# Thresholds and evaluations of its own for the second attention step of a four-layer graph network

## The reference

```python
S = adj + I;  Rf = S / rowsum(S);  Rb = S / colsum(S)[:, None]
Xf = Xb = Xa = X
for s in range(2):                       # the two attention steps
    logits = (Xa @ W1) @ W2 @ (Xa @ W3).T              # 3327 x 3327
    # row by row: keep the largest logits until their softmax mass reaches 0.9,
    # the softmax of these alone is A
    A = softmax(where(keep_top_mass(logits, 0.9), logits, -inf))
    Xf, Xb, Xa = Rf @ Xf, Rb @ Xb, A @ Xa
    Z += Xf @ U1[s] + Xb @ U2[s] + Xa @ U3[s]
out = layernorm(X + Z) * gamma + beta
```

## Time and profile before

| | us |
|---|---|
| median of three runs | 3657.98 |
| the profiled execution | 3658.36 |
| its span, first to last instruction | 3656.6 |
| busy: TensorE / VectorE / ScalarE / GpSimd | 3177.0 / 2622.1 / 1892.0 / 927.5 |

### The profile page before, as it was taken

The page is one execution under the profiler, slowest core; times in us unless marked ns, Lnnn a source line. Parts: engine busy times, 40 slices in busy tenths (PEclk is TensorE's granted clock), DMA queues, the critical chain, the costliest instruction groups (busy, mean ns, idle before and its releaser), DMA issues. The chain is left out here.

```text
span 3656.6 us, 40405 instructions
## 1 busy us (share of the span) xinstructions
PE 3177.0 (87%) x13264; PEld 2292.1 (63%) x13264; DVE 2622.1 (72%) x3768; ACT 1892.0 (52%) x2355; POOL 927.5 (25%) x2293
## 2 busy tenths in 40 slices
PE   4999899987999999989875887668799899996799
PEld 3788688875677676767642444334455555554588
DVE  6963400005989989998839999999999999999100
ACT  2211311117788787878744564546466566563100
POOL 1212411111122121221202233224233333234211
PEclk9999999988999999999987998889899999998899
DMA  6644444432122121222221111111122221222255
GB/s 246 216 156 135 129 152 156 156 116 65 52 66 61 55 67 56 60 57 60 63 71 40 55 48 45 49 35 54 46 80 57 76 80 58 76 76 79 73 191 178
DMA packets 142415, 328.48 MB, mean 90 GB/s; under 512 B 15456, under 2 KB 95392, under 8 KB 130976
## 3 DMA queue, kind: packets, MB, share of 16 engines
q1 hardware_dynamic: 142240, 326.31, 28.1%
HBM read 287.59 MB, written 38.67 MB: 89 GB/s over the span
## 5 line engine op out<-in xcount | busy, mean ns | idle before, releaser
L1345 DVE SCALAR_TENSOR_TENSOR U<-E,trial 128x3327 f32<-128x3327 f32 x208 | 777.7, 3739 | 0.2 <-issue 0.2
L878 PE MATMUL bank<-Hc,PT 128*128 128x256 f32 x2704 | 635.8, 387 | 53.8 <-ACT PT L1060 53.8
L878 PEld LDWEIGHTS bank<-Hc,PT 128*128 128x128 f32 x2704 | 520.5, 194 | 176.7 <-ACT PT L1060 77.5
L918 PE MATMUL bank<-big,adj 128*128 128x512 f32 x1352 | 612.3, 604 | 0.0
L1020 ACT ACTIVATE junk<-E,neg_c 128x3327 uint8<-128x3327 f32 x156 | 479.1, 3071 | 5.1
L1020 ACT ACTIVATE junk<-E,neg_3c 128x3327 uint8<-128x3327 f32 x156 | 478.3, 3066 | 0.0
L891 PE MATMUL tr<-ident,E 128*128 128x128 f32 x1352 | 203.7, 294 | 309.4 <-DVE E L1394 309.4
L918 PEld LDWEIGHTS bank<-big,adj 128*128 128x128 f32 x1352 | 254.7, 194 | 330.0 <-issue 327.4
L1060 ACT ACTIVATE PT<-tr 128x1024 f32<-128x1024 f32 x208 | 177.7, 854 | 472.2 <-PE tr L891 471.5
L891 PEld LDWEIGHTS tr<-ident,E 128*128 128x128 f32 x1352 | 174.8, 152 | 340.1 <-DVE E L1394 322.2
L918 PE MATMUL bank<-Hc,adj 128*128 128x256 f32 x1352 | 319.5, 388 | 1.2 <-ACT bias L1041 1.2
(11 more groups left out here) (232 smaller groups left out, 4424.1 us busy)
## 6 DMA issues: line engine op xcount, KB each, us to landing
adj<-adjT SPq DMA_DIRECT2D x131, 448.0 KB, 3.4
E<-adjT SPq DMA_DIRECT2D x32, 1664.0 KB, 6.9
adj<-adjT SPq DMA_DIRECT2D x104, 384.0 KB, 3.3
adj<-adjT SPq DMA_DIRECT2D x20, 1664.0 KB, 7.0
adj<-adjT SPq DMA_DIRECT2D x14, 1216.0 KB, 5.7
E<-adjT SPq DMA_DIRECT2D x13, 1216.0 KB, 5.7
xt<-xin SPq DMA_DIRECT2D x52, 128.0 KB, 5.5
x_d<-xn SPq DMA_DIRECT2D x52, 128.0 KB, 1.7
```

What stands on the lines that cost most here:

```text
L878: last = mm(axp[:, 0:D], PT[k % 2][:, h, i * P:(i + 1) * P], Hc[:, j], start=(k == 0 and h == 0 and i == 0), stop=(k == SLOTS - 1 and h == ...
L918: last = mm(agg[:, 0:w], adj[:, j], rhs[:, j], start=(j == 0), stop=False)
L1345: V_.scalar_tensor_tensor(out=U[:, 0:N], in0=e, scalar=point, in1=e, op0=ALU.is_ge, op1=ALU.mult, accum_out=found))
```

## The change

Step 2 gets fixed thresholds of its own, four in place of the shared three; it evaluates four times in place of five, and it aims at 4 elements short of the target in place of 3. Step 1 keeps its thresholds, evaluations and aim. The small tables of `bracket` exist once for each step.

```diff
-EVALS = (3, 5)
+EVALS = (3, 4)
-AIM = 3.0
+AIM = (3.0, 4.0)
-FIXED = (0.008, 0.03, 0.1)
-NF = len(FIXED)
+FIXED = ((0.008, 0.03, 0.1), (0.0029, 0.0064, 0.0142, 0.0315))
+NFS = tuple(len(f) for f in FIXED)
+SPLIT = ((0, 1, 3, 5, 6), (0, 2, 4, 7, 8))
...
+            summed = lambda t: 2 * (NFS[0] * min(t, NT) + NFS[1] * max(t - NT, 0))
...
                         def fixed(t, lo, hi):
-                            sums = [(func, c, acc_) for c in range(NF) for func, acc_ in ((ACT.Relu, over), (ACT.Sign, sign))]
+                            step = t // NT
+                            sums = [(func, c, acc_) for c in range(NFS[step])
+                                    for func, acc_ in ((ACT.Relu, over), (ACT.Sign, sign))]
...
-                                    fixed(F, 0, 1)
+                                    fixed(F, *SPLIT[F // NT][0:2])
...
-                                        fixed(F, 1, 3)
+                                        fixed(F, *SPLIT[F // NT][1:3])
...
-                                        fixed(F, 3, 5)
+                                        fixed(F, *SPLIT[F // NT][2:4])
...
-                                        fixed(F, 5, 2 * NF)
+                                        fixed(F, *SPLIT[F // NT][3:5])
...
-                            pool.wait_ge(fixed_done, 2 * NF * (t + 1))
+                            pool.wait_ge(fixed_done, summed(t + 1))
...
-                                then(V_.tensor_scalar(sc[:, 0:1], point, AIM, tgt, ALU.mult, ALU.subtract),
+                                then(V_.tensor_scalar(sc[:, 0:1], point, AIM[step], tgt, ALU.mult, ALU.subtract),
```

More of the change, by code:

```diff
@@ L660, in build @@
             rz = ab("rz", [P, 4])
[L661 to L671, removed]
+            over = ab("over", [P, 2, max(NFS)])
+            sign = ab("sign", [P, 2, max(NFS)])
+            neg_c = [ab(f"neg_c{r}", [P, n]) for r, n in enumerate(NFS)]
+            neg_3c = [ab(f"neg_3c{r}", [P, n]) for r, n in enumerate(NFS)]
+            half_c = [ab(f"half_c{r}", [P, n]) for r, n in enumerate(NFS)]
+            half_nc = [ab(f"half_nc{r}", [P, n]) for r, n in enumerate(NFS)]
+            table = [ab(f"table{r}", [P, n + 2, 3]) for r, n in enumerate(NFS)]
+            ft = [ab(f"ft{r}", [P, 2, n]) for r, n in enumerate(NFS)]
+            met = [ab(f"met{r}", [P, n + 2]) for r, n in enumerate(NFS)]
+            pick = [ab(f"pick{r}", [P, n + 1]) for r, n in enumerate(NFS)]
+            both = [ab(f"both{r}", [P, 2, n + 1, 3]) for r, n in enumerate(NFS)]
             share = ab("share", [P, 5])
@@ L1013, in fixed @@
                         def fixed(t, lo, hi):
-                            sums = [(func, c, acc_) for c in range(NF) for func, acc_ in ((ACT.Relu, over), (ACT.Sign, sign))]
+                            step = t // NT
+                            sums = [(func, c, acc_) for c in range(NFS[step])
+                                    for func, acc_ in ((ACT.Relu, over), (ACT.Sign, sign))]
                             for m in range(lo, hi):
                                 func, c, acc_ = sums[m]
-                                if 2 * NF * t + m >= 1:
-                                    act.wait_ge(fixed_done, 2 * NF * t + m)
-                                less, scale = (neg_3c, 3.0) if func == ACT.Sign else (neg_c, 1.0)
+                                if summed(t) + m >= 1:
+                                    act.wait_ge(fixed_done, summed(t) + m)
+                                less, scale = (neg_3c[step], 3.0) if func == ACT.Sign else (neg_c[step], 1.0)
                                 go(junk[:, 0:N], E[:, t % 3, 0:N], func, bias=less[:, c:c + 1], scale=scale,
@@ L1161, in _ @@
                         tt = G_.tensor_tensor
[L1162 to L1167, removed]
+                        values = []
+                        for r in range(2):
+                            n = NFS[r]
+                            values += [(table[r][:, 0], 0.0), (table[r][:, n + 1, 0:1], 1.5), (table[r][:, n + 1, 1:3], 0.0),
+                                       (met[r][:, 0:1], 1.0), (met[r][:, n + 1:n + 2], 0.0)]
+                            for i, value in enumerate(FIXED[r]):
+                                c, _ = between_floats(value)
+                                values += [(table[r][:, i + 1, 0:1], c), (half_c[r][:, i:i + 1], c / 2),
+                                           (half_nc[r][:, i:i + 1], c * N / 2)]
                         for i, value in enumerate((P_NUC, 1 - P_NUC, -P_NUC, -1.0, 1 - 2.0 ** -24)):
@@ L1175, in bracket @@
                         def bracket(t):
-                            par = t % 2
+                            par, step = t % 2, t // NT
+                            NF = NFS[step]
                             n = [0]
@@ L1186, in bracket @@
                             lo, hi = ends2[:, par, 0], ends2[:, par, 1]
-                            mid = table[:, 1:NF + 1]
-                            pool.wait_ge(fixed_done, 2 * NF * (t + 1))
+                            mid = table[step][:, 1:NF + 1]
+                            pool.wait_ge(fixed_done, summed(t + 1))
                             if t >= 2:
                                 pool.wait_ge(probs_ready, t - 1)
-                            then(tt(ft[:, 0], sign[:, par], half_c[:], ALU.mult),
-                                 tt(ft[:, 1], over[:, par], half_nc[:], ALU.add),
+                            then(tt(ft[step][:, 0], sign[:, par, 0:NF], half_c[step][:], ALU.mult),
+                                 tt(ft[step][:, 1], over[:, par, 0:NF], half_nc[step][:], ALU.add),
@@ L1194, in bracket @@
                                  tt(tgt, Zs[:, par:par + 1], share[:, 0:1], ALU.mult),
-                                 tt(table[:, 0, 1:2], Zs[:, par:par + 1], share[:, 1:2], ALU.mult),
-                                 tt(table[:, NF + 1, 1:2], Zs[:, par:par + 1], share[:, 2:3], ALU.mult))
-                            then(tt(mid[:, :, 2], ft[:, 0], ft[:, 1], ALU.add))
+                                 tt(table[step][:, 0, 1:2], Zs[:, par:par + 1], share[:, 1:2], ALU.mult),
+                                 tt(table[step][:, NF + 1, 1:2], Zs[:, par:par + 1], share[:, 2:3], ALU.mult))
@@ L1198, in bracket @@
+                            then(tt(mid[:, :, 2], ft[step][:, 0], ft[step][:, 1], ALU.add))
                             then(tt(mid[:, :, 1], mid[:, :, 2], tgt.to_broadcast([P, NF]), ALU.subtract),
                                  tt(below, tgt, share[:, 4:5], ALU.mult),
-                                 G_.tensor_scalar(met[:, 1:NF + 1], mid[:, :, 2], tgt, None, ALU.is_ge))
+                                 G_.tensor_scalar(met[step][:, 1:NF + 1], mid[:, :, 2], tgt, None, ALU.is_ge))
                             for i in range(2, NF + 1):
-                                then(tt(met[:, i:i + 1], met[:, i:i + 1], met[:, i - 1:i], ALU.mult))
@@ L1203, in bracket @@
[L1203 to L1207, removed]
+                                then(tt(met[step][:, i:i + 1], met[step][:, i:i + 1], met[step][:, i - 1:i], ALU.mult))
+                            then(tt(pick[step][:], met[step][:, 0:NF + 1], met[step][:, 1:NF + 2], ALU.subtract))
@@ L1208, in bracket @@
+                            w = pick[step][:].unsqueeze(2).to_broadcast([P, NF + 1, 3])
+                            then(tt(both[step][:, 0], table[step][:, 0:NF + 1], w, ALU.mult),
+                                 tt(both[step][:, 1], table[step][:, 1:NF + 2], w, ALU.mult))
                             for i in range(1, NF):
-                                then(tt(both[:, :, 0], both[:, :, 0], both[:, :, i], ALU.add))
-                            then(tt(ends2[:, par], both[:, :, 0], both[:, :, NF], ALU.add))
+                                then(tt(both[step][:, :, 0], both[step][:, :, 0], both[step][:, :, i], ALU.add))
@@ L1212, in bracket @@
+                            then(tt(ends2[:, par], both[step][:, :, 0], both[step][:, :, NF], ALU.add))
                             then(tt(sp_[:, 0:1], lo[:, 1:2], hi[:, 1:2], ALU.subtract),
@@ L1294, in _ @@
                         V_.memset(ones8[:], 1.0)
[L1295 to L1298, removed]
+                        for r in range(2):
+                            for i, value in enumerate(FIXED[r]):
+                                c, three_c = between_floats(value)
+                                V_.memset(neg_c[r][:, i:i + 1], -c)
+                                V_.memset(neg_3c[r][:, i:i + 1], -three_c)
                         V_.memset(flag[:], 0.0).then_inc(search, 1)
```

## The result

The changed kernel takes **3735.6 us** (median of 4 runs, 3730.05 to 3737.45) against 3658.45 before: a ratio of **1.0208**, 95% interval 1.0195 to 1.0221. It is slower by 77 us, where 60 us faster was forecast. The profiled execution is the shortest of the four, 3730.05 us, so the sums taken from its trace come to about 72 us and not 77.

A forecast was written before the change was run, and what follows sets the result against it. VectorE was taken to bound step 2, with GpSimd's bracket close behind. −137 evaluations + 69 waits + 7 start + 3 collision = −58, −60 after rounding: 3658 − 60 = 3598 us, range 3564 to 3642.

The forecast's parts named there:

- The number of rounds: Extraction-loop rounds in step 2, taken as unchanged at 51; forecast case 45 to 58, about −94 us at 45, −20 at 57.
- Rival 1: Four evaluations leave rows needing more extraction rounds in step 2; slower, 3690 us at 66 rounds; chance 0.14.
- In the walk a round is worth 6.3 us on average, not 8.83: Tile-by-tile reckoning of step 2: an extraction round costs 6.3 us net, because it takes a wait away.
- L: Time from end of tile T to start of tile T+2 that the ScalarE-GpSimd chain allows; 52.6 to 56.5 us.
- the third sum of slot 2: Added fixed sum on ScalarE in slot 2, where it works without a gap: 3.2 us on L.
- Bracket +0.5: GpSimd's bracket, one more turn in each of two loops: 0.5 us on L, range zero to 1.0.
- Slot-0 sum: Second fixed sum on ScalarE in slot 0, fitting its 3.16 us wait for TensorE's transposes: 0.2 us on L.
- Rival 2: Slot-0 sum not hidden, both sums in L (6.4 us): 3627 us, or 3681 if the pipeline's period grew; chance 0.10.
- The evaluations, −137: One VectorE evaluation removed in each of step 2's 26 tiles, 5.28 us each, the slow fourth staying: −137 us.
- The collision with L1275, +3: GpSimd's 256-wide addition before the bracket held under VectorE's last pass in two two-round tiles: 3 us, ends 0 and 22.
- The start, +6.9: Start of step 2, tile 26 waiting uncovered for two added sums and the longer bracket: 6.4 + 0.5 = 6.9 us.
- The waits: VectorE's waits between tiles of step 2, from 22 to 91 us, eating 69 of the 137 us saved.

The follow-up runs named there:

- The pairs of runs: Thresholds as moved (factor 3) against as written (1.0625): changed kernel 3735.6 and 3657.59 us; three low thresholds, four evaluations, aim 5: 3637.12 and 3583.24 us.
- the fastest kernel: Kernel before with three low thresholds for step 2 (0.003, 0.0102, 0.0347, factor 1.0625), four evaluations, aim 5, no added sums: 3583.24 us, 0.9777.

## Why the prediction was wrong

**The number of rounds is the step that failed.** The prediction took 51, "the row nearest", with a grid "reaching down to 0.0029". That grid isn't in the program: `between_floats` had moved three of four thresholds up by 10 to 35%. At the written values the count is 56, inside the forecast's own 45 to 58; at the moved ones it is 65, where 51 were taken. The 9 rounds between them are 9 x 8.83 = 79 us, and the two kernels stand 78 apart; that the two agree so well is partly luck, since waits and start also differ. The moved values could have been read before the run: the helper stands in the kernel and its arithmetic decides the value that the engine gets. The count that follows from them could not be read from any row, as the prediction says itself. Rival 1 had the right sign and mechanism (at 66 rounds 3690 us), with a chance of 0.14, and it named the missing evaluation as the cause. The experiments share that out: evaluation alone 90 rounds, the change 65, the thresholds where they were meant 56, and with three low thresholds 57. So the missing evaluation does cost rounds, and thresholds and aim as meant win all but 5 of them back.

**"In the walk a round is worth 6.3 us on average, not 8.83"** gives 3686 at 65 rounds (3690 at 66) where 3735 came. Of the 14 rounds eight fell on two tiles, four more in each, where only the first can take a wait away. And the waits, at 102, were above the 91 foreseen with 51 rounds, because L was larger than worked out. (That 102 is so near 91 is luck: three one-round tiles in place of eight, and an L of 60.2 in place of 56.5. The prediction's own ends of the range also follow from its 6.3 only to within 4 us.) The pairs of runs give 54 us for 7 rounds and 78 for 9.

**L, "from 52.6 to 56.5"**, came out at 60.2 in rounds that weren't late themselves. The terms: the third sum of slot 2, given 3.2, took 2.9 with five evaluations; no run has it alone with four. Bracket +0.5: right, 5.6 to 6.2. Slot-0 sum, "I take 0.2": right with five evaluations (0.8 at most), wrong in this kernel, 3.9. With 52.5 undisturbed, 52.5 + 3.2 + 0.6 + 3.9 = 60.2. The prediction priced the sum against TensorE, and it does fit into that wait. What it missed is that GpSimd's layernorm chain starts behind the same sum, and that with the fifth evaluation gone the mask pass starts 1.6 us earlier than that evaluation did, before the chain is through. Both halves are shown: the sum moved away brings L to 56.1 where nothing else collides, the fifth evaluation given back brings it to 57. Rival 2 had the size (both sums in L) by another cause.

**The evaluations, −137:** −143, right, though not as argued: the slow fourth did not simply stay, part of it moved into the mask pass. **The collision with L1275, +3:** L1283, as it is called here, is held in 4 of the 26 tiles, and the bracket of tiles 41, 46, 47 and 48 then starts 1.9 us after the last sum in place of 0.1. **The start, +6.9:** 10.8, of which 3.2 were there at the end of step 1 already and the sums and bracket make 7.6. That 3.2 also comes and goes between the experiments (step 1 ends between 1855.1 and 1860.8), and I leave its cause open. **The waits:** with 65 rounds the prediction's own rules and L = 56.5 give about 54 us of waits and 29 us slower; with L = 60.2 they give 91 and 66, and the trace has 102 and 72. So of the way from −60 to +72 some 90 us are rounds and some 40 are L. Moving the one sum took 39 us away.

**What would have shown it wrong** was named: MAX8 at 60 or more, and L at 59 or above. Both came.

## What to carry to other kernels

- Where a constant goes through a helper before it reaches an engine, work out the value that arrives. Here three constants out of four were not what the line said, and it cost 78 us.
- A loop that runs until the slowest of 128 rows is done is set by single rows. Its count can't be taken over from the old setting when the search before it changes; it is the first thing to bound, not the last.
- Work put into an engine's idle time can still delay what another engine takes from behind it. Ask who reads the next result in that queue, not only what the engine waits for.

## What the runs showed of the hardware

- A GpSimd operation of one column is held as long as a wide one: L1235, 128x1, took 3.20 us when it started 0.5 us into VectorE's 3.68 us pass with two SBUF inputs, against 0.19 to 0.22 in the 10 of 26 tiles where it was free. VectorE pays too when GpSimd comes first: in this trace the pass then takes 4.03 to 4.23. The Trainium skill (SBUF — State Buffer, "SBUF: two separate sides") has this as an exclusive lock held for a whole instruction; the trace agrees, and shows that in a chain of tiny operations each one that starts inside such a pass costs the rest of the pass: the layernorm chain above was held at L1235 and again at L1243 in one round.
- Granted clock of TensorE over step 2: 0.89 with the changed kernel, 0.91 before, where TensorE is busy 79% of the stretch in place of 81%; 0.948 over the whole of the fastest kernel, 0.939 over that of before. It is lower where TensorE waits more; no run here holds the waiting still and moves the clock, so what it adds itself stays open.
